# A twice normed input: both norms of the second attention from one set of statistics

## The chip, the cores and the metric

The kernel runs on one core of a Trainium2 chip. Its engines work side by side: TensorE (PE) multiplies, VectorE (DVE), ScalarE (ACT) and GpSimd (POOL) do elementwise work, SyncE (SP) issues the transfers. Each engine takes its instructions in the order of the program, and waits on semaphores that others raise. The time is that of one execution on the device in microseconds; a comparison goes by the median of the runs.

## What is computed

x has 8 batches of 256 rows of 256 numbers. Four blocks follow one another, each adding to x: an attention of x to a context, a block with self attention and a choice among 8 experts, a second attention to the context, and a block of small experts. The change is in the second one:

```python
def _layernorm(x, axis=-1, eps=1e-05):
    m = jnp.mean(x, axis=axis, keepdims=True)
    v = jnp.var(x, axis=axis, keepdims=True)
    return (x - m) / jnp.sqrt(v + eps)
...
    def _L0_ffn_ref(x, ln1_g, ln1_b, ...):
        hn = _layernorm(x, ln1_g, ln1_b)
        q = (hn @ wq + bq)...
        ...
        x = x + (o @ wo + bo)
        ...
        return x + moe.reshape(b, s, h)
    x = x + _L0_ffn_ref(_layernorm(x, axis=-1), ...)
```

So the rows of x are normed (call this y, to which the attention's result is added), and y is normed once more for the projections to queries, keys and values.

## The kernel before

All work stands in one list, `STEPS`, of small steps with a batch number; every engine walks through the list and does its part of each step. Batches 0 to 7 are the first attention, 8 to 15 the self attention, 16 to 23 the second attention to the context. `pipeline` lays out the list: each batch has a few chains of steps with hand written due times (`T_SELF` for the chain that starts a self attention batch), and the attention units of the current batch (`sc` scores, `pv` values) are the clock that the due times refer to. PE's own order is the list's.

The steps that matter here:
- `na` (`norm_stats`, line 1015): on DVE two BN_STATS and two BN_AGGR (one for each tile of 128 rows) and a TENSOR_SCALAR that adds eps to both variances (`ve`); on POOL (line 1312) one TENSOR_TENSOR with the exponent -0.5 in `mhalf`, which makes the two reciprocal roots `rs`. The numbers lie in a ring of three small tiles, `mv`.
- `nb` (`norm_apply`, line 1029): on DVE two TENSOR_SCALAR, (source - mean) * root. `norm_io` gives source and destination. For a self attention batch n, `("nb", n, 0)` writes y from x and `("nb", n, 1)` writes z from y; z is what PE turns (`zt`) and ACT and PE make queries (`qp`), keys (`kp`) and values (`vp`) of.
- `qs` and `ks`: a projection is split into three bf16 parts; POOL subtracts (`rqa`, line 1327), DVE casts (`spa`, line 1050), POOL subtracts again (line 1334), and SP sends the parts to the stacks of queries and keys (line 1473).
- `mx`: PE multiplies queries and keys for the row maxima (line 604), DVE reduces them (`nma`, line 1072). Their results and those of most other steps share a ring of three PSUM banks, so PE's next step often waits for the reduction three back.
- `p0`, `ps`, `p1`, `p2`: reciprocal of the softmax sums (`La`, line 1088), its splitting into bf16 parts (`Lpa`, lines 1094 to 1100), the product that spreads it (line 652), the output projection (line 661) and DVE's addition of it to x or y (line 1113).
- `of`: POOL adds the output bias to x or y (line 1340).

Before, `("nb", n, 0)` and `("na", n, 1)` stand in one segment of the chain, and `("nb", n, 1)` in the next, whose due time is 0.02 of a batch later.

## Time and profile before

| | us |
|---|---|
| median of 3 runs | 949.85 |
| lowest and highest | 948.77, 954.06 |
| the profiled execution | 945.36 |
| its span | 943.6 |

The span by stage, from the busy times by stretch (us; granted clock as a share of 2.4 GHz):

| stretch | what runs | PE busy | DVE busy | POOL busy | clock |
|---|---|---|---|---|---|
| 0 to 126 | first attention, start | 77.5 | 66.6 | 39.4 | 0.84 |
| 126 to 427 | self attention, and the first one's end | 255.4 | 227.9 | 94.3 | 0.94 |
| 427 to 627 | the eight experts | 169.9 | 40.8 | 25.0 | 0.93 |
| 627 to 870 | second attention to the context | 173.3 | 158.8 | 80.5 | 0.75 |
| 870 to 943.6 | small experts, end | 63.7 | 48.2 | 3.6 | 0.96 |

Within the second stage PE is busy for 30.5 of 38 us (126 to 164), 58.6 of 66 (164 to 230) and 77.8 of 87 (230 to 317).

How to read the rows further down: start in us from the span's start, length in us, engine, line of the kernel, operation, destination <- sources, shapes, how many were merged in the row ("x2"), and in brackets how long the engine was idle before it and what ended that. A start can lie a little before the end of the row ahead, since instructions overlap in their pipeline.

### The profile page before, as it was taken

How to read it: one execution, taken by the hardware profiler on the slowest of the kernel's cores; microseconds unless marked ns; L12 is line 12 of the kernel's file. 1: busy time of each engine (PE TensorE's matmuls, PEld its weight loads, DVE VectorE, ACT ScalarE, POOL GpSimd, SP SyncE). 2: the span in 40 equal slices, each digit the busy share in tenths (PEclk: the TensorE clock that was granted, in tenths of full speed). 3: DMA queues.
4: the chain of work that ended last, by engine and by line, in shares of the span. 5: the costliest groups of instructions: out<-in, count | busy, mean ns of one | idle time of the engine just before them, and what ended most of it. 6: DMA issues, size and time to landing. Idle time of an engine off the chain costs nothing.

```text
span 943.6 us, 15777 instructions
## 1 busy us (share of the span) xinstructions
PE 739.9 (78%) x5815; PEld 548.4 (58%) x5815; DVE 542.2 (57%) x1319; ACT 344.2 (36%) x627; POOL 242.7 (26%) x242
## 2 busy tenths in 40 slices
PE   3657878889988999930999999935477768887898
PEld 2434655556555655420999999924354545565775
DVE  3546588987788687442111221125558889465585
ACT  1324454545454455510222222204044444543313
POOL 1513233333333331312111110026233542212000
PEclk9768898999999999965999999978578898665999
DMA  4959364855555484336455566246936442060202
GB/s 149 123 76 199 67 92 71 117 83 82 68 119 63 82 139 155 114 122 145 177 187 198 169 175 181 91 103 75 113 58 90 82 73 42 13 280 13 86 0 91
DMA packets 66191, 102.94 MB, mean 109 GB/s; under 512 B 20078, under 2 KB 56366, under 8 KB 60958
## 3 DMA queue, kind: packets, MB, share of 16 engines
q1 hardware_dynamic: 63699, 96.75, 47.9%
q0 software_dynamic: 2416, 5.19, 3.0%
q8 instruction: 47, 0.77, 0.4%
q14 instruction: 29, 0.24, 0.1%
HBM read 56.29 MB, written 7.28 MB: 67 GB/s over the span
## 4 chain that ended last, share of the span: by engine, by line
PE 53%; DVE 21%; DMA 10%; issue 5%; ACT 5%; POOL 3%; SPq 3%; DVEq 0%; POOLq 0%; ACTq 0%
PE PS L723 9%; PE U L734 8%; PE U L641 6%; PE MB L574 6%; PE MB L661 4%; PE PS L627 4%; PE MB L604 3%; DVE R L1276 3%; DVE nma L1072 3%; DMA La<-Uba 2%; SPq L1473 2%; DMA y<-yb,pos 2%; PE PS L778 2%; DMA QKa<-mTa 2%; PE MB L590 2%
## 5 line engine op out<-in xcount | busy, mean ns | idle before, releaser
L1072 DVE TENSOR_REDUCE nma<-MB 128x2 f32<-128x512 f32 (+1 forms) x192 | 123.9, 671 | 36.9 <-PE MB L604 35.2
L899 ACT ACTIVATE Pa<-PS 128x1024 f32<-128x1024 f32 (+1 forms) x96 | 97.4, 1023 | 65.8 <-PE PS L627 65.2
L604 PE MATMUL MB<-QKa 99*128 99x120 bf16 (+1 forms) x512 | 73.4, 259 | 29.5 <-DVE nma L1072 18.0
L641 PE MATMUL U<-Pa,Vaa 128*32 128x256 f32 (+1 forms) x768 | 91.7, 403 | 0.9 <-ACT Pa L899 0.7
L723 PE MATMUL PS<-mzT,mw 128*128 128x128 f32 x736 | 87.6, 278 | 1.8 <-ACT mzT L921 1.8
L723 PEld LDWEIGHTS PS<-mzT,mw 128*128 128x128 f32 x736 | 85.6, 195 | 2.4 <-issue 2.3
L734 PE MATMUL U<-mw,mdT 128*128 x368 | 83.3, 380 | 2.3 <-DVE mdT L1224 2.3
L1232 DVE TENSOR_TENSOR yt<-U,mb 128x256 f32<-128x256 f32 x23 | 9.8, 424 | 122.7 <-PE U L734 122.7
L1318 POOL TENSOR_TENSOR mv<-mv,vec 128x2 f32<-128x2 f32 x48 | 34.1, 711 | 178.4 <-DVE mv L1027 178.4
L604 PEld LDWEIGHTS MB<-QKa 99*128 99x128 bf16 x512 | 39.3, 103 | 61.9 <-DVE nma L1072 26.8
L734 PEld LDWEIGHTS U<-mw,mdT 128*128 128x128 f32 x368 | 68.2, 190 | 11.0 <-issue 2.7
L627 PE MATMUL PS<-QKa 101*128 101x256 bf16 (+1 forms) x384 | 59.7, 279 | 4.9 <-DMA QKa<-mTa 4.9
L921 ACT ACTIVATE mzT<-MB,vec 128x128 f32<-128x128 f32 x46 | 18.5, 454 | 116.5 <-PE MB L707 116.5
L574 PE MATMUL MB<-zTa,W 128*128 128x256 f32 x192 | 47.9, 393 | 7.5 <-ACT zTa L842 6.1
L1327 POOL TENSOR_TENSOR rqa<-tqa,spa 128x512 f32<-128x512 f32 (+1 forms) x28 | 32.6, 1166 | 81.1 <-ACT tqa L881 38.9
L1365 POOL DMA_INDIRECT zt<-hb,rows_of x23 | 21.7, 945 | 121.8 <-PE MB L707 117.0
L641 PEld LDWEIGHTS U<-Pa,Vaa 128*32 128x32 f32 (+1 forms) x768 | 31.0, 111 | 32.5 <-issue 15.4
L1072 DVE TENSOR_REDUCE nmb<-MB 128x4 f32<-128x480 f32 x64 | 40.7, 651 | 14.4 <-PE MB L604 13.7
L627 PEld LDWEIGHTS PS<-QKa 101*128 101x128 bf16 (+1 forms) x384 | 37.8, 113 | 17.1 <-issue 8.1
L899 ACT ACTIVATE Pb<-PS 120x1024 f32<-120x1024 f32 x32 | 32.7, 1021 | 34.8 <-PE PS L627 34.6
L574 PEld LDWEIGHTS MB<-zTa,W 128*128 128x128 f32 x192 | 35.0, 192 | 16.7 <-ACT zTa L842 7.7
L1334 POOL TENSOR_TENSOR spa<-rqa,spa 128x512 bf16<-128x512 f32 (+1 forms) x28 | 32.5, 1159 | 43.8 <-DVE spa L1050 43.8
(202 smaller groups left out, 1381.1 us busy)
## 6 DMA issues: line engine op xcount, KB each, us to landing
mw<-in_mw SPq DMA_DIRECT2D x31, 1024.0 KB, 5.6
QKa<-spa SPq DMA_DIRECT2D x144, 128.0 KB, 4.7
Qb<-spb SPq DMA_DIRECT2D x48, 128.0 KB, 5.5
Oa<-Uba SPq DMA_DIRECT2D x16, 256.0 KB, 3.8
v<-in_v SPq DMA_DIRECT2D x1, 4096.0 KB, 13.5
v<-in_v SPq DMA_DIRECT2D x4, 1024.0 KB, 11.7
W<-in_W SPq DMA_DIRECT2D x3, 1280.0 KB, 6.6
yb<-yt SPq DMA_DIRECT2D x23, 128.0 KB, 1.7
```

The costliest lines, as they stand in the source:

```text
L574: i = e.matmul(b[:, 256 * half:256 * half + cols], w[:, k, 128 * half:128 * half + 128], rhs[:, k, :], start=k == 0, stop=k == 1)
L604: i = e.matmul(b[:, keys * j:keys * j + keys], Q[0:99, h0 + j, 128 * qt:128 * qt + 128], K[0:99, h0 + j, 0:keys], start=True, stop=True)
L627: i = e.matmul(ps[0:keys, c:c + 256], K[0:101, h, keys * kt:keys * kt + keys], Q[0:101, h, :], start=True, stop=True)
L641: i = e.matmul(U[32 * j:32 * j + 32, 256 * gg:256 * gg + 256], V[0:keys, kt, 8 * half + 4 * gg + j, :], p[0:keys, c:c + 256], start=kt == ...
L661: i = e.matmul(b[:, 256 * tt:256 * tt + 256], o[:, half, 128 * tt:128 * tt + 128], W.o[:, half, :], start=half == 0, stop=half == 1)
L723: i = e.matmul(ps[:, 128 * f:128 * f + 128], w[:, k, 128 * f:128 * f + 128], zz[:, k, :], start=k == 0, stop=k == 1)
L734: i = e.matmul(U[:, 0:256], mdT[j % 2][:, f, :], w2[:, bass.ds(expert[j], 1), f, :], start=f == 0, stop=f == 7)
L899: e.activation(p[0:keys, :], ps[0:keys, :], ACT.Exp, scale=0.25).then_inc(sems["exp"], 1)
L1072: e.tensor_reduce(A.nm[qt][:, h0:h0 + heads], b[:, 0:heads * keys].rearrange("p (h s) -> p h s", h=heads), AX.X, ALU.max, negate=True).the ...
L1318: e.tensor_tensor(rs[r][:, 0:2], ve[r][:, 0:2], mhalf[:, 0:2], ALU.pow).then_inc(sems["rs"], 1)
L1327: e.tensor_tensor(r, f32, hi, ALU.subtract).then_inc(sems["split_r"], 1)
L1334: e.tensor_tensor(low, A.rq[k % 2][:, :, 0:cols], mid_, ALU.subtract).then_inc(sems["split_l"], 1)
```

## The change

With the mean m and the variance v of a row of x, y = (x - m) / sqrt(v + eps) has mean 0 and variance v / (v + eps). Its norm is therefore (x - m) / sqrt(v * (1 + eps) + eps^2). The change takes statistics of x alone for a self attention batch, and makes both y and z from x with them. `("na", n, 1)` is gone; `("na", n, 0)` has one more TENSOR_SCALAR on DVE, which makes the second pair of `ve`, and POOL's power works on four numbers a row instead of two. z (`nb` with 1) now comes first, in the segment where y was made, and y (`nb` with 0) in the next, where z was. `stats_done` and `applied` give the semaphore values that the constant 5 and `k - 2` gave before; `twofold` names the norms that have two users. POOL's bias addition waits for both. All else in the list keeps its place.

```diff
--- before.py
+++ after.py
@@ -83,7 +83,7 @@
             task(at(T_KEYS[L][1:]), [("vp", n)])
             task(at(T_CROSS), [("na", n, 0)], [("nb", n, 0)], [("zt", n)], [("qp", n)], [("qs", n)], [("qd", n), ("of", n)])
         else:
-            task(at(T_SELF), [("na", n, 0)], [("nb", n, 0), ("na", n, 1)], [("nb", n, 1)], [("zt", n)], [("qp", n)],
+            task(at(T_SELF), [("na", n, 0)], [("nb", n, 1)], [("nb", n, 0)], [("zt", n)], [("qp", n)],
                  [("qs", n), ("kp", n)], [("qd", n), ("ks", n)], [("kr", n), ("kd", n), ("vp", n), ("of", n)])
         per = 4 if cross(n) else 8
         segments = []
@@ -246,6 +246,7 @@
 
 PAIRS = Ring(2, score_users())
 NORM = {s[1:]: k for k, s in enumerate(s for s in STEPS if s[0] == "na")}
+NORMS = list(NORM)
 HT = Ring(2, [(s, ("logits", s[1] - 7) if s[0] == "gt" else ("choice", s[1] - 15)) for s in STEPS if s[0] in ("gt", "ft")])
 
 
@@ -296,6 +297,25 @@
 KEY_SENT, KEY_ROWS, KEY_BEFORE = key_uses()
 LOW = {(s[0][0] + "p", s[1]): k for k, s in enumerate(s for s in STEPS if s[0] in ("qs", "ks"))}
 NB_AT = {s[1:]: k + 1 for k, s in enumerate(s for s in STEPS if s[0] == "nb")}
+
+
+def twofold(n, i):
+
+
+    return i == 0 and not cross(n)
+
+
+def stats_done(k):
+
+    return sum(6 if twofold(*s) else 5 for s in NORMS[:k])
+
+
+def applied(k):
+
+    n, i = NORMS[k]
+    return max(NB_AT[n, i], NB_AT[n, 1] if twofold(n, i) else 0)
+
+
 Z_STEPS = [s[1] for s in STEPS if s[0] == "zt"]
 
 
@@ -347,11 +367,11 @@
     vec = g0.new("vec", [128, 160])
     cst = g0.new("cst", [128, 176])
     lo = g0.new("lo", [128, 2, 128], BF)
-    mhalf = vec[:, 136:138]
+    mhalf = vec[:, 136:140]
     st = g0.ring("st", 3, [128, 2, 6])
-    mvs = g0.ring("mv", 3, [128, 8])
+    mvs = g0.ring("mv", 3, [128, 12])
     mv = [t[:, 0:4].rearrange("p (n m) -> p n m", n=2) for t in mvs]
-    ve, rs = [t[:, 4:6] for t in mvs], [t[:, 6:8] for t in mvs]
+    ve, rs = [t[:, 4:8] for t in mvs], [t[:, 8:12] for t in mvs]
     oh = g0.new("oh", [128, NT, 8])
     gw = g0.new("gw", [128, 2, 8])
     hT = g0.ring("ghT", 2, [128, 2, 256])
@@ -532,7 +552,7 @@
         if i == 0:
             ready = ((f"d_x{b}", 16), ("resid", NO["p2"].get((n - 8,), 0)), ("back", b + 1))[layer(n)]
         else:
-            ready = (None, ("nb", NORM[n, 0] + 1), ("resid", NO["p2"].get((n,), 0)), ("resid", NO["p2"].get((n,), 0)))[i]
+            ready = ("resid", NO["p2"].get((n,), 0))
         if (i == 0 and cross(n)) or i == 1:
             z = att(n).z[z_of(n) % 2]
             dst = [z[:, k, :] for k in range(2)]
@@ -540,7 +560,7 @@
             dst = [Yz[b % 2][:, k, :] for k in range(2)]
         else:
             dst = ys
-        return (xs if i in (0, 3) else ys), dst, ready
+        return (ys if i == 2 else xs), dst, ready
 
     def normed(n):
         return "nb", NB_AT[n, 0 if cross(n) else 1]
@@ -1016,18 +1036,23 @@
             k = NORM[n, i]
             r = k % 3
             src, _, ready = norm_io(n, i)
+            done = stats_done(k)
             g.wait_ge(*ready)
-            g.wait_ge("nb", k - 2)
+            if k >= 3:
+                g.wait_ge("nb", applied(k - 3))
             for t in range(2):
                 e.bn_stats(st[r][:, t, :], src[t]).then_inc(sems["na"], 1)
             for t in range(2):
-                g.wait_ge("na", 5 * k + 1 + t)
+                g.wait_ge("na", done + 1 + t)
                 e.bn_aggr(mv[r][:, t, :], st[r][:, t, :]).then_inc(sems["na"], 1)
-            g.wait_ge("na", 5 * k + 4)
+            g.wait_ge("na", done + 4)
             e.tensor_scalar(ve[r][:, 0:2], mv[r][:, 0:2, 1], EPS, None, ALU.add).then_inc(sems["na"], 1)
+            if twofold(n, i):
+                e.tensor_scalar(ve[r][:, 2:4], mv[r][:, 0:2, 1], 1.0 + EPS, EPS * EPS, ALU.mult, ALU.add
+                                ).then_inc(sems["na"], 1)
 
         def norm_apply(n, i):
-            k = NORM[n, i]
+            k = NORM[n, 0 if i == 1 else i]
             r = k % 3
             src, dst, _ = norm_io(n, i)
             if (i == 0 and cross(n)) or i == 1:
@@ -1040,7 +1065,8 @@
                 g.wait_ge("fl", n - 17)
             g.wait_ge("rs", k + 1)
             for t in range(2):
-                o = e.tensor_scalar(dst[t], src[t], mv[r][:, t, 0:1], rs[r][:, t:t + 1], ALU.subtract, ALU.mult)
+                w = 2 + t if i == 1 else t
+                o = e.tensor_scalar(dst[t], src[t], mv[r][:, t, 0:1], rs[r][:, w:w + 1], ALU.subtract, ALU.mult)
             o.then_inc(sems["nb"], 1)
 
         def split_mid(what, n):
@@ -1313,9 +1339,11 @@
             k = NORM[n, i]
             r = k % 3
             g.wait_ge("mhalf", 1)
-            g.wait_ge("nb", k - 2)
-            g.wait_ge("na", 5 * k + 5)
-            e.tensor_tensor(rs[r][:, 0:2], ve[r][:, 0:2], mhalf[:, 0:2], ALU.pow).then_inc(sems["rs"], 1)
+            if k >= 3:
+                g.wait_ge("nb", applied(k - 3))
+            g.wait_ge("na", stats_done(k + 1))
+            w = 4 if twofold(n, i) else 2
+            e.tensor_tensor(rs[r][:, 0:w], ve[r][:, 0:w], mhalf[:, 0:w], ALU.pow).then_inc(sems["rs"], 1)
 
         def split_rest(what, n):
             A, k = att(n), SPLIT[what, n]
@@ -1336,7 +1364,7 @@
         def offset(n):
             res = (x if cross(n) else y)[:, two(n % NB), :]
             g.wait_ge(f"d_W{layer(n)}", 16)
-            g.wait_ge(*normed(n))
+            g.wait_ge("nb", max(NB_AT[n, 0], normed(n)[1]))
             e.tensor_tensor(res, res, over(LW[layer(n)].bo, 2, 1), ALU.add).then_inc(sems["offset"], 1)
 
         def add_y(n):
```

DVE at the start of batch 8, before (`x` and `y` are the residual tiles, `za` is z, `st` the statistics, `mv` the ring of means, variances and roots):

```order
L1072 TENSOR_REDUCE nma_85<-MB 128x4
L1081 CAST Mha_90<-nma_86 128x16
L1083 TENSOR_TENSOR Mha_90<-nma_86,Mha_90 128x16
L1043 TENSOR_SCALAR y<-x,mv_61 128x256 x2
L1022 BN_STATS st_56<-y 128x6 x2
L1025 BN_AGGR mv_59<-st_56 128x2 x2
L1027 TENSOR_SCALAR mv_59<-mv_59 128x2
L1050 CAST spa_107<-rqa_103 128x512
L1043 TENSOR_SCALAR za_96<-y,mv_59 128x256 x2
L1072 TENSOR_REDUCE nma_85<-MB 128x4
```

and in the changed kernel:

```order
L1098 TENSOR_REDUCE nma_85<-MB 128x4
L1107 CAST Mha_90<-nma_86 128x16
L1109 TENSOR_TENSOR Mha_90<-nma_86,Mha_90 128x16
L1069 TENSOR_SCALAR za_96<-x,mv_61 128x256 x2
L1076 CAST spa_107<-rqa_103 128x512
L1069 TENSOR_SCALAR y<-x,mv_61 128x256 x2
L1098 TENSOR_REDUCE nma_85<-MB 128x4
```

The pair that writes za has moved up to the first pair's place and reads x; the statistics of y are gone, and the pair that writes y stands behind the cast.

POOL there, before (`mv` is the power, `rqa` and `spa` the two subtractions of a split):

```order
L1318 TENSOR_TENSOR mv_61<-mv_61,vec 128x2
L1327 TENSOR_TENSOR rqa_103<-tqa_101,spa_107 128x512
L1318 TENSOR_TENSOR mv_59<-mv_59,vec 128x2
L1334 TENSOR_TENSOR spa_107<-rqa_103,spa_107 128x512
L1340 TENSOR_TENSOR x<-x,W_74 128x512
```

and in the changed kernel:

```order
L1346 TENSOR_TENSOR mv_61<-mv_61,vec 128x4
L1355 TENSOR_TENSOR rqa_103<-tqa_101,spa_107 128x512
L1362 TENSOR_TENSOR spa_107<-rqa_103,spa_107 128x512
L1368 TENSOR_TENSOR x<-x,W_74 128x512
```

The second power, between the two subtractions, is gone, and the first has four columns.

DVE at batch 13, where the splitting of the softmax sums (`La`, `Lpa`) stands between the two pairs, before:

```order
L1088 RECIPROCAL La_82<-La_82 32x128
L1043 TENSOR_SCALAR y<-x,mv_59 128x256 x2
L1022 BN_STATS st_57<-y 128x6 x2
L1025 BN_AGGR mv_60<-st_57 128x2 x2
L1027 TENSOR_SCALAR mv_60<-mv_60 128x2
L1094 CAST Lpa_94<-La_82 32x128
L1096 TENSOR_TENSOR La_82<-La_82,Lpa_94 32x128
L1098 CAST Lpa_94<-La_82 32x128
L1100 TENSOR_TENSOR Lpa_94<-La_82,Lpa_94 32x128
L1050 CAST spa_104<-rqa_102 128x512
L1043 TENSOR_SCALAR za_97<-y,mv_60 128x256 x2
L1072 TENSOR_REDUCE nma_85<-MB 128x2
```

and in the changed kernel:

```order
L1114 RECIPROCAL La_82<-La_82 32x128
L1069 TENSOR_SCALAR za_97<-x,mv_60 128x256 x2
L1120 CAST Lpa_94<-La_82 32x128
L1122 TENSOR_TENSOR La_82<-La_82,Lpa_94 32x128
L1124 CAST Lpa_94<-La_82 32x128
L1126 TENSOR_TENSOR Lpa_94<-La_82,Lpa_94 32x128
L1076 CAST spa_104<-rqa_102 128x512
L1069 TENSOR_SCALAR y<-x,mv_60 128x256 x2
L1098 TENSOR_REDUCE nma_85<-MB 128x2
```

Here the four instructions of the sums come right behind the pair that writes za. PE's, ACT's and SP's orders are the same in both kernels.

## Rows read from the trace of the kernel before

**Rows 1.** Timeline of DVE at batch 8 (start us, us, operation, idle before).

```profile
132.86 1.65 DVE L1043 TENSOR_SCALAR y<-x,mv 128x256 f32<-128x256 f32 x2
134.55 0.75 DVE L1022 BATCH_NORM_STATS2 st<-y 128x6 f32<-128x256 f32 x2
...
135.55 0.17 DVE L1027 TENSOR_SCALAR mv<-mv 128x2 f32<-128x2 f32 x1
135.63 0.42 DVE L1050 CAST spa<-rqa 128x512 bf16<-128x512 f32 x1
136.70 2.42 DVE L1043 TENSOR_SCALAR za<-y,mv 128x256 f32<-128x256 f32 x2 [0.65 <-POOL mv L1318]
139.05 0.64 DVE L1072 TENSOR_REDUCE nma<-MB 128x4 f32<-128x480 f32 x1
```

**Rows 2.** The same of POOL at batch 8, and its first bias addition to y.

```profile
135.80 0.80 POOL L1318 TENSOR_TENSOR mv<-mv,vec 128x2 f32<-128x2 f32 x1 [1.43 <-DVE mv L1027]
136.56 1.15 POOL L1334 TENSOR_TENSOR spa<-rqa,spa 128x512 bf16<-128x512 f32 x1
137.67 1.30 POOL L1340 TENSOR_TENSOR x<-x,W 128x512 f32<-128x512 f32 x1
...
162.77 1.27 POOL L1340 TENSOR_TENSOR y<-y,W 128x512 f32<-128x512 f32 x1
```

**Rows 3.** Timeline at batch 13: DVE, last row POOL.

```profile
238.98 0.75 DVE L1022 BATCH_NORM_STATS2 st<-y 128x6 f32<-128x256 f32 x2
...
240.06 0.21 DVE L1094 CAST Lpa<-La 32x128 bf16<-32x128 f32 x1
...
241.22 0.43 DVE L1050 CAST spa<-rqa 128x512 bf16<-128x512 f32 x1
241.57 1.57 DVE L1043 TENSOR_SCALAR za<-y,mv 128x256 f32<-128x256 f32 x2
243.05 0.68 DVE L1072 TENSOR_REDUCE nma<-MB 128x2 f32<-128x512 f32 x1
...
241.73 1.25 POOL L1334 TENSOR_TENSOR spa<-rqa,spa 128x512 bf16<-128x512 f32 x1 [0.75 <-DVE spa L1050]
```

**Rows 4.** Timeline at batch 10: DVE, then POOL.

```profile
168.61 0.73 DVE L1043 TENSOR_SCALAR y<-x,mv 128x256 f32<-128x256 f32 x2
...
170.45 0.42 DVE L1050 CAST spa<-rqa 128x512 bf16<-128x512 f32 x1
...
173.77 1.27 DVE L1072 TENSOR_REDUCE nma<-MB 128x2 f32<-128x512 f32 x2
...
167.53 0.70 POOL L1318 TENSOR_TENSOR mv<-mv,vec 128x2 f32<-128x2 f32 x1 [3.48 <-DVE mv L1027]
169.17 1.18 POOL L1327 TENSOR_TENSOR rqa<-tqa,spa 128x512 f32<-128x512 f32 x1 [0.95 <-ACT tqa L884]
```

**Rows 5.** Timeline of PE: rows that carry a wait, batches 8, 9, 10, 13.

```profile
139.75 0.38 PE L604 MATMUL MB<-QKa 99*128 99x120 bf16 x4 [3.20 <-DVE nma L1072]
...
159.60 1.99 PE L590 MATMUL MB<-W,zTa 128*128 128x256 f32 x8 [0.57 <-DVE x L1113]
...
172.11 0.60 PE L604 MATMUL MB<-QKa 99*128 99x256 bf16 x4 [1.39 <-issue]
...
243.78 3.50 PE L661 MATMUL MB<-W,Oa 128*128 128x256 f32 x8 [1.48 <-DVE nma L1072]
```

**Rows 6.** Timeline at batches 11 and 12: DVE, DVE, PE.

```profile
196.82 0.69 DVE L1113 TENSOR_TENSOR x<-x,MB 128x512 f32<-128x512 f32 x1 [0.17 <-PE MB L661]
...
216.09 1.27 DVE L1072 TENSOR_REDUCE nma<-MB 128x2 f32<-128x512 f32 x2
...
216.27 1.90 PE L661 MATMUL MB<-W,Oa 128*128 128x256 f32 x8
```

**Rows 7.** Second attention to the context: busy times by stretch (engines, clock, DMA); one product, ns min/median/max.

```profile
627.00:850.00 223.00, 157.84 (x1204) 110.92 (x1206) 147.62 (x329) 88.64 (x149) 77.45 (x75) 0.77 0.50 94
...
L574 PE MATMUL MB<-zTb,W x40: 378/379/748, 642.7 to 707.5; 128*128 128x256 f32 x40
```

## Prediction

> **What bounds the kernel now.** I read the busy time by stretch first, then TensorE's (PE's) rows that carry a wait, then the rows of VectorE (DVE) and GpSimd (POOL) at each place the diff touches. The change is confined to the second stretch of the table above, the self attention of batches 8 to 15, whose eight double norms start between 132.9 and 299.4 us. The other stretches stand before or behind it and are not touched; in its three parts named under the table, PE is busy for 80 to 89%. So the question is how much of the work taken from DVE lies on the way to PE's next product.
>
> Batch 8 is the clearest place [rows 1]. DVE makes y from x with the first norm (132.86), takes statistics of y (from 134.55), adds eps (135.55), does an unrelated cast (135.63), and makes za, the second norm of y, from 136.70 on: between the cast and za it stands 0.65 us, until POOL's power (135.80 plus 0.80) is there [rows 2]. Only then can it do the maximum at 139.05. PE has no other work: its row at 139.75 shows 3.20 us of waiting for that maximum [rows 5]. The pair za takes 2.42 us, where an undisturbed pair of this shape takes 0.73 (168.61) [rows 4]: it runs while POOL has two subtractions or additions back to back, 136.56 and 137.67 [rows 2].
>
> Batch 13 shows the other pattern [rows 3]. There the four splitting steps of the softmax sums stand between, so the power is ready in time, and the pair za meets one POOL operation (241.73) before it gets through: from the cast's start (241.22) to the next maximum (243.05) 1.83 us pass. PE waits 1.48 us for that maximum in its row at 243.78 [rows 5]; the rows at 275.88 and 304.95, for batches 14 and 15, carry the same 1.48.
>
> **What is removed.** Per batch two BN_STATS, two BN_AGGR and one TENSOR_SCALAR go. They occupy DVE from 134.55 to 135.63, that is 1.08 us [rows 1]; in batch 13 from 238.98 to 240.06, again 1.08 [rows 3]. The stop for the second power goes as well: the two reciprocal roots come out of one POOL operation, issued over 3 us earlier in batch 8. Eight POOL operations of 0.70 to 0.80 us go, which nobody but DVE waited for.
>
> **What moves.** za takes the place of the first pair, and y that of the second, behind the cast. The first pair keeps its price. The second now starts right behind the cast, with no power in POOL's queue, which is how batches 13 to 15 already run, so I price it by their 1.83 us from cast to maximum. In batch 8 the same distance is 135.63 to 139.05, 3.42 us [rows 1]: 1.59 are saved. In batch 10 it is 170.45 to 173.77, 3.32 us [rows 4], and the rows of batch 9 have the same 3.32: 1.49 are saved in each.
>
> **Batch by batch**, what DVE gains and what PE can take of it:
> - Batch 8: 1.08 + 1.59 = 2.67 us. PE stood 3.20 us for it, so all of it counts: **2.67**.
> - Batch 9: DVE gains 1.08 + 1.49 = 2.57, but PE's own product keeps it busy, and behind it the row at 159.60 waits only 0.57 for DVE's residual addition [rows 5], and one before it 0.18 for a maximum. I take both, **0.75**; the bounds are 0.57 and 2.57.
> - Batch 10: the cast needs POOL's subtraction, 169.17 plus 1.18 = 170.35 [rows 4], so it can only move from 170.45 to about 170.40; 0.05 + 1.49 = 1.54. DVE runs from there almost without a stop, and PE's row at 172.11 has 1.39 us of waiting that no engine is named for. I read it as the landing of batch 8's keys, sent after a cast that DVE now reaches sooner. **1.5**.
> - Batches 11 and 12: the next thing that DVE must do is an addition for which PE's product is late: at 196.82 it waits 0.17 for PE in spite of everything; in batch 12 the product runs from 216.27 to 218.17, while DVE comes to the same addition over maxima that start at 216.09 and take 1.27 and a reciprocal of about 0.9 [rows 6], so just in time. What DVE gains (1.73 and 0.7 by the same working) ends in a wait for PE. **0**.
> - Batches 13, 14, 15: no stop for the power, the cast-to-maximum distance is unchanged, so 1.08 each, and PE stands 1.48 for each: **3.24**.
>
> Sum 2.67 + 0.75 + 1.5 + 3.24 = 8.16 us.
>
> **What is added.** One TENSOR_SCALAR on 128x2 beside the one that adds eps. The existing one is 0.17 us long and the next instruction starts 0.08 behind it when it does not depend on it (135.55, 135.63) [rows 1]. Eight such are 0.6 us of DVE at most 1.4; about half of them lie where DVE is what PE waits for: 0.3. The power works on four numbers a row, not two. No row has that shape: its bounds are 0.70, if its time is all fixed cost, and 1.40, if it is all work. The tightest place is batch 10, power at 167.53, pair at 168.61 [rows 4]: 0.70 hides, 1.40 would hold the pair 0.3 us. I take nothing, since 0.70 for two numbers against 1.15 for the 512 of 136.56 says fixed cost. The addition of the output bias to y (POOL) now waits for y behind za; the first comes at 162.77, 24 us after both pairs [rows 2], so this costs nothing. Rings with fewer users and earlier frees cost nothing.
>
> So **8.16 - 0.3 = 7.9 us**. The profiled execution took 945.36 us, so it would take 937.5. The median of the runs is 949.85; the profiled one is 4.5 below it, and the same saving in each gives **941.9**.
>
> **Where the pair y could come out dearer.** In rows 3 the pair starts 0.16 us ahead of POOL's subtraction and meets one POOL operation; in batch 8 POOL was first and both halves of the pair waited, one operation each. If POOL came first in batches 8 to 10, only the stop of 0.65 would be saved behind the cast, not 1.59 and 1.49: 0.94 + 0.84 + 0.84 = 2.6 less, a gain of 5.3. The Trainium skill (SBUF — State Buffer, Who interferes with whom) says that a VectorE instruction in a two-port mode and a GpSimd one share a port pair that the first to start holds for its whole length; with the pair at the front in all three batches that gives the sum above, with POOL at the front the smaller gain. The trace agrees with it on both patterns, 2.42 and 1.57 us for the pair. I keep 1.83 because both POOL's operation and the pair are released by the same cast, and POOL needs a signal for it while DVE only goes on.
>
> **The rivals.**
> - *The saving is taken back by others* (0 to 4.5 us gained, 945.4 to 949.9). PE is busy for most of this stage; wherever it comes early, it may find the next keys not landed, as in the row at 172.11, or ScalarE not done. If batches 9 and 10 give nothing and 13 to 15 give half, 2.67 + 1.6 = 4.3 us, 945.6. For it: two of eight batches give nothing already in my own reckoning. Against: the 1.48 and 3.20 us are waits for DVE alone.
> - *More comes through* (12.1 us, 937.8). Batch 9 gives its full 2.57 and batches 11 and 12 their 1.73 and 0.7: 7.9 + 1.8 + 2.4 = 12.1. It needs PE's waits on ScalarE to fall too. Against: DVE's own rows wait for PE there.
> - *Slower by the clock of the second attention to the context.* That stretch runs at a mean granted clock of 0.77 [rows 7], switching between the levels 1.2 and 2.4 GHz, and the same product takes 0.379 us at one and up to 0.748 at the other [rows 7]. The change moves this stage by some 8 us against whatever sets the switching. It decides once about 8 us of PE work more fall to the lower level, some 16 us of its 223, a mean clock near 0.70; at 0.65 the result is 5 to 6 us slower, 955. For it: a clock that goes up and down here many times. Against: fewer waits ahead of it, and no work changed in it.
> - That the change does not do what it says can be left out: the order of DVE shows the five instructions gone and PE's order is the same.
>
> **Chances.** Forecast, 5 to 9.5 us gained: 0.48. Taken back: 0.27. More: 0.16. Slower: 0.09. A measurement can tell about 0.5%, 4.7 us, from no change. Faster by more than that: the forecast, more, and a sliver of the second case, 0.66. Same: 0.27. Slower, at a little under the last case: 0.07. The range reaches from the large gain to a gain of 1.4: 937.5 to 948.5; below it and above it I leave about 0.2.
>
> **What will show it.** In the profile after: no statistics of y in front of za, and no wait of DVE for POOL's power in batches 8 to 12; PE's wait of 3.20 in batch 8 down to about 0.5; the three waits of 1.48 down to 0.4; cast to maximum 1.8 us in batches 8 to 10, and the power of 128x4 near 0.7 us. The end of the stage (the last product of the router, near 423 us) should be 8 us earlier, and the stretch behind it as long as before. The forecast is wrong if those waits turn up under ScalarE or a transfer, if the pair y takes 2.4 us, or if the second half is longer at a lower clock.

## The result and the profile after

The changed kernel took 939.14 us (median of 4 runs, 933.67 to 941.93) against 949.31 before (4 runs, 947.75 to 954.06); the ratio is 0.9889, with a 95% interval of 0.9854 to 0.9923. A second set of runs of the same kernel gave 0.993 (0.9895 to 0.9966; 12 runs against 35). Both intervals lie below 1; the medians are 10.2 and 6.3 us apart, and the forecast was 7.9. The two profiled executions of the changed kernel, though, have spans of 931.9 and 944.8 us, so a single profile's total says little here. What can be compared is how long a piece of the program takes in each profile.

DVE at batch 8 in the profile after, the columns as ahead of the prediction; it answers [rows 1]:

```profile
132.85 0.73 DVE L1069 TENSOR_SCALAR za<-x,mv 128x256 f32<-128x256 f32 x2
134.62 0.43 DVE L1076 CAST spa<-rqa 128x512 bf16<-128x512 f32 x1 [1.05 <-POOL rqa L1355]
134.97 1.57 DVE L1069 TENSOR_SCALAR y<-x,mv 128x256 f32<-128x256 f32 x2
136.46 0.65 DVE L1098 TENSOR_REDUCE nma<-MB 128x4 f32<-128x480 f32 x1
```

The pair that writes za stands first and is undisturbed, 0.73 us. The cast now waits 1.05 us for POOL's first subtraction, which nothing hides any more; the pair y takes 1.57 us, and the maximum follows 1.8 us behind the cast instead of 3.42. The power with four columns, and the first row of PE behind all this, which was [rows 5]'s 139.75 with its 3.20 us:

```profile
129.65 1.02 POOL L1346 TENSOR_TENSOR mv<-mv,vec 128x4 f32<-128x4 f32 x1 [6.25 <-DVE mv L1051]
...
137.16 0.38 PE L624 MATMUL MB<-QKa 99*128 99x120 bf16 x4 [0.63 <-DVE nma L1098]
```

The power takes 1.02 us, between the bounds of 0.70 and 1.40, and delays nobody here. At batch 10, where it is tightest, it ends at 164.34 and the pair starts at 164.45, after 0.11 us of idle time. PE's wait is 0.63. At batch 13 (DVE, POOL, PE; [rows 3] and the last of [rows 5] answer to it):

```profile
235.27 1.36 DVE L1069 TENSOR_SCALAR za<-x,mv 128x256 f32<-128x256 f32 x2
236.56 0.21 DVE L1120 CAST Lpa<-La 32x128 bf16<-32x128 f32 x1
...
237.68 0.43 DVE L1076 CAST spa<-rqa 128x512 bf16<-128x512 f32 x1
238.02 1.57 DVE L1069 TENSOR_SCALAR y<-x,mv 128x256 f32<-128x256 f32 x2
239.51 0.68 DVE L1098 TENSOR_REDUCE nma<-MB 128x2 f32<-128x512 f32 x1
...
238.18 1.26 POOL L1362 TENSOR_TENSOR spa<-rqa,spa 128x512 bf16<-128x512 f32 x1 [2.02 <-DVE spa L1076]
...
240.25 1.99 PE L681 MATMUL MB<-W,Oa 128*128 128x256 f32 x8 [0.59 <-DVE nma L1098]
```

The splitting of the sums starts right behind the pair za. PE's wait for the maximum fell from 1.48 to 0.59 us, and its projection in the same row from 3.50 to 1.99. That second fall was in no term of the sum. The waits for the maximum in batches 14 and 15 fell less, from 1.48 to 1.04 and 0.98 (269.67 and 297.54); 0.4 was forecast for all three.

At batch 10, on PE, where [rows 5] has 1.39 us at 172.11:

```profile
168.97 1.01 PE L624 MATMUL MB<-QKa 99*128 99x256 bf16 x4 [2.59 <-issue]
```

This wait has grown to 2.59 us. It was to shrink.

**One table for all kernels.** Each kernel's first product of the softmax sums with `Lpa` (line 652 before; it belongs to batch 4, and stands at 125 to 130 us) is taken as zero, since the start alone differs by 5 us between executions. Times in us. "To batch 13" ends at the same product of batch 10's sums, six products further; in the profile of before it stands at 241.25 us, 2.5 ahead of the wait of 1.48 in batch 13, so it holds what batches 8 to 12 gave. "13 to 15" is from there to the product three further, past the third such wait; "experts" is the first product of the experts' stage; "rest" is what follows the last expert product to the end of the span.

| kernel | first maxima product of batch 8 | to batch 13 | "13 to 15" | experts | rest | ratio to before (95%) |
|---|---|---|---|---|---|---|
| before | 47.09 | 116.2 | 90.0 | 323.5 | 323.3 | |
| changed, first profile | 43.89 | 113.2 | 84.2 | 315.9 | 318.7 | 0.9889 (0.9854, 0.9923) |
| changed, `again` | 45.34 | 115.9 | 84.3 | 318.1 | 323.6 | 0.993 (0.9895, 0.9966) |
| `y_first` | 45.41 | 113.2 | 84.2 | 315.0 | 322.6 | 0.9914 (0.9878, 0.995) |
| `dummy_stats` | 46.17 | 116.2 | 89.9 | 324.6 | 323.0 | 0.9998 (0.9965, 1.0031) |
| `second_power` | 46.12 | 115.5 | 84.2 | 318.5 | 322.9 | 0.9976 (0.9946, 1.0005) |
| `only_13_15` | 46.75 | 115.3 | 84.2 | 317.3 | 323.2 | 0.9956 (0.9926, 0.9986) |
| `only_8_10` | 45.22 | 113.6 | 89.7 | 320.5 | 317.3 | 0.9956 (0.9917, 0.9995) |
| `only_11_12` | 46.62 | 115.8 | 90.2 | 323.5 | 323.4 | 1.0013 (0.9978, 1.0048) |
| `keys_sooner` | 45.53 | 113.3 | 84.2 | 314.7 | 317.9 | one run, 937.75 us |
| `y_later` | 43.96 | 113.5 | 84.9 | 318.3 | 323.2 | 0.993 (0.9891, 0.997) |
| `eight_sooner` | 44.10 | 114.9 | 87.8 | 320.8 | 324.0 | 0.9928 (0.9887, 0.9968) |
| `both_moves` | 42.88 | 112.1 | 84.4 | 314.2 | 324.2 | 0.9925 (0.9891, 0.9959) |

The column "rest" has two values, 317 to 319 and 322.6 to 324.2, in kernels whose work there is the same, and the changed kernel shows both. The 5 us lie in the last two batches of the second attention to the context: between the products of the last three batches' softmax sums pass 11.5 and 16.9 us in the first profile after and 13.2 and 20.5 in `before` and in `again`, and the clock differs there. So the difference between the two executions of the changed kernel is not the change's. The experts' stage itself, from its first product to its last, is in no column and has two values too: 171.7 to 172.3 us in `before`, the first profile after and the three kernels with the new way in some batches only, and 174.1 to 174.8 in the eight others, the second execution of the changed kernel among them. Whether the change makes the longer value more frequent, no run here shows; `before` was profiled once.

Up to the experts, the two executions of the changed kernel are 7.6 and 5.4 us ahead of before. They differ by 2.7 us ahead of batch 13. There the granted clock is at 1.2 GHz for 13.7 us in `again`, counted from the product at zero (two of the stretches begin at 175.5 and 192.5 us), and for 6.8 us in the first profile (one begins at 168.6). In `before`, `y_first`, `y_later`, `keys_sooner`, `eight_sooner` and the three kernels with the new way in some batches only it is 6.8 us as well, in `dummy_stats` and `second_power` 10.2, in `both_moves` 3.4. So of single profiles a difference under some 3 us in that column says little unless these times are the same; the column "13 to 15" repeats within 0.1.

### The profile page after: what moved, and what is told of

Read it like the earlier page. It is cut to its first block, busy times and chain, and to the rows that moved or that the text cites. A ratio compares the mean times of both kernels' runs of the same rounds, so it can differ in the third digit from the quotient of the medians.

```text
span 931.9 us, 15736 instructions
## 1 busy us (share of the span) xinstructions
PE 731.7 (79%) x5815; PEld 543.8 (58%) x5815; DVE 532.9 (57%) x1287; ACT 344.3 (37%) x627; POOL 240.7 (26%) x234
## 4 chain that ended last, share of the span: by engine, by line
PE 54%; DVE 20%; DMA 8%; issue 5%; ACT 5%; SPq 3%; POOL 3%; DVEq 0%; POOLq 0%; ACTq 0%
PE PS L743 9%; PE U L754 9%; PE U L661 7%; PE MB L594 6%; PE MB L681 4%; PE PS L647 4%; PE MB L624 3%; DVE R L1302 3%; DVE nma L1098 2%; SPq L1501 2%; DMA y<-yb,pos 2%; DMA QKa<-mTa 2%; PE MB L610 2%; PE MB L833 2%; PE PS L798 2%
## 5 line engine op out<-in xcount | busy, mean ns | idle before, releaser
L1346 POOL TENSOR_TENSOR mv<-mv,vec 128x2 f32<-128x2 f32 (+1 forms) x40 | 31.1, 777 | 156.3 <-DVE mv L1049 105.4
L661 PEld LDWEIGHTS U<-Pa,Vaa 128*32 128x32 f32 (+1 forms) x768 | 30.7, 110 | 31.7 <-issue 14.2
```

Source lines behind the costliest of these rows:

```text
L661: i = e.matmul(U[32 * j:32 * j + 32, 256 * gg:256 * gg + 256], V[0:keys, kt, 8 * half + 4 * gg + j, :], p[0:keys, c:c + 256], start=kt == ...
L1346: e.tensor_tensor(rs[r][:, 0:w], ve[r][:, 0:w], mhalf[:, 0:w], ALU.pow).then_inc(sems["rs"], 1)
```

## The experiments

### Which part of the removal counts

`again` is the changed kernel.

> The changed kernel once more, unaltered. In its first profile the stretch up to the experts' start was 7.1 to 8.3 us shorter than before (PE's last router transposition at 409.09 instead of 417.39), and the rest of the span 3.4 to 4.6 us shorter as well, although no work there is changed. Theory A (the change is worth what its stage shows, about 8 us, and the rest is how the clock of the second context attention fell in that one execution): the stage ends again near 409 to 410, the total lands 7 to 11 us under the kernel before, and the rest of the span differs from 522 us by a few us. Theory B (the later stages gain too): the rest is again near 522 us and the total 10 to 12 us under.

It took 942.37 us against 948.7. Its stage ended 5.8 us earlier than the kernel before, counted from the product at zero (277.4 instead of 283.2), or 5.4 at the experts, and its rest was 323.6: theory A, though the gain in the total, 6.3 us, lies below its 7 to 11. The expected absolute times were of no use, since the start shifts.

`dummy_stats` puts the five DVE instructions back, with unused results:

```diff
-            task(at(T_SELF), [("na", n, 0)], [("nb", n, 1)], [("nb", n, 0)], [("zt", n)], [("qp", n)],
+            task(at(T_SELF), [("na", n, 0)], [("nb", n, 1), ("dm", n)], [("nb", n, 0)], [("zt", n)], [("qp", n)],
...
+        def dummy(n):
...
+                e.bn_stats(s[t], x[:, 2 * (n % NB) + t, :]).then_inc(sems["dummy"], 1)
...
+                e.bn_aggr(m[:, t, :], s[t]).then_inc(sems["dummy"], 1)
...
+            e.tensor_scalar(vec[:, 156:158], m[:, 0:2, 1], EPS, None, ALU.add).then_inc(sems["dummy"], 1)
```

> The changed kernel with five VectorE instructions put back behind each pair that writes z: two BN_STATS and two BN_AGGR and a TENSOR_SCALAR into unused columns, read by nobody. No second power on GpSimd. It prices the removed instructions apart from the removed stop. My theory: they cost 1.08 us per batch, in full in batches 8, 10, 13, 14 and 15 and not in 11 and 12, so the stage ends 5 us later than in the changed kernel (near 414), total about 944. The rival (the stop for the power was what mattered, the five instructions run in the shadow of PE): the stage ends within 1.5 us of 409. In batch 8 PE's first maxima product stands at 138.2 by my theory, at 137.2 by the rival.

With the five back, nothing measurable is left: 948.29 us against 948.7, where about 944 was expected, and the experts start 1.1 us later than before, although the stop for the second power is gone and the second pair is cheaper. Part of that can be the clock: ahead of batch 13 this profile has 3.4 us more at 1.2 GHz than before, which at half the speed is at most 1.7 us. DVE at batch 8:

```profile
134.29 1.69 DVE L1069 TENSOR_SCALAR za<-x,mv 128x256 f32<-128x256 f32 x2
135.91 0.74 DVE L1077 BATCH_NORM_STATS2 vec<-x 128x6 f32<-128x256 f32 x2
136.57 0.29 DVE L1080 BATCH_NORM_AGGREGATE vec<-vec 128x2 f32<-128x6 f32 x2
136.89 0.17 DVE L1082 TENSOR_SCALAR vec<-vec 128x2 f32<-128x2 f32 x1
136.97 0.42 DVE L1088 CAST spa<-rqa 128x512 bf16<-128x512 f32 x1
137.31 1.57 DVE L1069 TENSOR_SCALAR y<-x,mv 128x256 f32<-128x256 f32 x2
138.80 0.64 DVE L1110 TENSOR_REDUCE nma<-MB 128x4 f32<-128x480 f32 x1
```

The instructions cost 1.06 us, from 135.91 to 136.97, as priced, and from the cast on the batch is as cheap as in the changed kernel (1.83 us to the maximum, 3.42 before). PE's first maxima product behind it stands 0.94 us later than in the changed kernel, counted from the zero, as expected, but by the rows the reason is the first pair, which took 1.69 us beside POOL's subtraction: after a pair of 0.73 the five would have been done at about 136.0, and the cast needs that subtraction, which ends at 135.84. So the price of 1.59 us for stop and contention was right in its place, and worth nothing measurable at the end. That contradicts the share of it in my sum: of 7 to 8 us I expected 5 to go, and all went.

`second_power` is the other half: statistics once, but y first, one TENSOR_SCALAR where the five stood, and the second power on POOL ahead of z.

```diff
+            task(at(T_SELF), [("na", n, 0)], [("nb", n, 0), ("pw", n)], [("nb", n, 1)], [("zt", n)], [("qp", n)],
...
+        def second_variance(n):
...
+            e.tensor_scalar(ve[r][:, 2:4], mv[r][:, 0:2, 1], 1.0 + EPS, EPS * EPS, ALU.mult, ALU.add
...
+        def second_power(n):
...
+            e.tensor_tensor(rs[r][:, 2:4], ve[r][:, 2:4], mhalf[:, 2:4], ALU.pow).then_inc(sems["pw_a"], 1)
```

> Statistics of x alone, as in the changed kernel, but order and power as before: y first, then one TENSOR_SCALAR for the second variance where the five instructions stood, then the second power on GpSimd, then z behind the cast. It takes away four instructions (about 1.0 us per batch) and keeps the stop. My theory: batches 8 and 10 gain only about 1 us each, 13 to 15 about 1.0 each, so the stage ends near 412.5 (4 to 5 us before the kernel before, 3 to 4 behind the changed one). The rival (the stop is worth nothing because it hides under PE): it ends near 409, like the changed kernel. In batch 8 the maximum starts 3.4 us after the cast, not 1.8.

Of DVE at batch 8:

```profile
135.38 0.43 DVE L1080 CAST spa<-rqa 128x512 bf16<-128x512 f32 x1 [1.23 <-POOL rqa L1364]
136.10 2.43 DVE L1068 TENSOR_SCALAR za<-x,mv 128x256 f32<-128x256 f32 x2 [0.30 <-POOL mv L1355]
138.45 0.65 DVE L1102 TENSOR_REDUCE nma<-MB 128x4 f32<-128x480 f32 x1
```

The stop is 0.30 us here and the pair takes 2.43, with POOL busy throughout; cast to maximum is 3.07 us, where 3.4 was expected. It comes to batch 13 at 115.5, about where `again` does, so nothing can be read from that; and its stage ends at 276.5, between the two executions of the changed kernel (274.8 and 277.4), which decides for neither theory. But batches 13 to 15 take 84.2 us, as in the changed kernel. At the experts it is 5.0 us ahead; its total is 2.3 us ahead with an interval that reaches from 5.1 ahead to 0.5 behind, so the total alone settles nothing. The four removed instructions are all that counts in batches 13 to 15.

`y_first` swaps the two pairs back.

> The changed kernel with only the order of the two pairs swapped back: y in the first place, z in the second, behind the cast. Nobody takes z before PE's transposition, whose place in PE's order is some 5 us later. My theory: the order is worth nothing, the stage ends within 0.5 us of the changed kernel's 409.1. The rival (z's being ready earlier is part of the gain): it ends 1 us or more later.

It comes to batch 13 at 113.2 and takes 84.2 us from there, like the first profile of the changed kernel; the ratio is 0.9914. The order of the two is worth nothing, as expected: both pairs read x, so neither needs the other.

### Batch by batch

The changed kernel with the new way for some batches only (`ONCE` holds them; the others are as before):

```diff
+ONCE = (13, 14, 15)
...
+            first_, second_ = ([("nb", n, 1)], [("nb", n, 0)]) if n in ONCE else ([("nb", n, 0), ("na", n, 1)], [("nb", n, 1)])
...
-    return i == 0 and not cross(n)
+    return i == 0 and n in ONCE
```

> Only batches 13, 14 and 15 take both norms from x; batches 8 to 12 are as before. Times are counted from PE's first product of softmax sums with Lpa (batch 4, near 125 us), since the start varies by some us. Theory A (the granted clock doubles the gain here: the waits of 1.5 us that go had each been followed by a half-clock stretch): up to the product of batch 10 it is like before, 116.2 us, and the last one is at 277.4 instead of 283.2, 5.8 us earlier, against the 3.24 of the prediction; the half-clock stretches that the profile of before records at 254.9 and 316.3 are gone. Theory B (the gain there is only the instructions): 280.0, and the two half-clock stretches stay.

> Only batches 8, 9 and 10 take both norms from x. Counted from the same product. The prediction's sum would be 4.9 us. Theory A (in batches 8 to 10 the transfers of the first self attention queries and keys take it back: 15.7 us from the first send of the queries of batch 8 to the first maxima product of batch 8, whatever the engines do): 0.4 to 3.1 us at the product of batch 10 (116.2 before), and the half-clock stretches near 255 and 316 stay, so the total is 0 to 3 us under before. Theory B: 4 us or more.

> Only batches 11 and 12 take both norms from x. My theory: nothing, since VectorE waits for PE's projection there anyway: the product of batch 10 at 116.2 us and the last at 283.2 from the first, each within 0.5, total within 1 us of before. The rival (the slack of the two is smaller than it looks): 1 us or more at the product of batch 10.

Batches 13 to 15 alone take "13 to 15" from 90.0 to 84.2 us, 5.8, against the 3.24 of the sum. Batches 11 and 12 alone give 0.0 at the experts. Batches 8 to 10 alone come to batch 13 at 113.6, against 116.2, 115.3 and 115.8 in the three profiles with the old way in these batches and the same 6.8 us at 1.2 GHz: 1.7 to 2.7 us, against the 4.9 of the sum. Five of the six profiles with the whole change in batch 8 and its old place lie between 113.2 and 113.6, only `again`, with its 13.7 us at the lower clock, at 115.9. In all three runs the first of the two theories holds for the gain. The places that the expectations give for the stretches at 1.2 GHz were read wrongly: counted from the start of the span, as all rows here are, they begin at 243.4 and 304.9 us in the profile of before, not at 254.9 and 316.3, so at the ends of the waits at 243.78 and 304.95. The wait at 275.88 has none.

**Why 5.8.** PE at batch 13 in `dummy_stats`, where the wait is as before, and in `only_13_15`:

```profile
245.21 3.56 PE L681 MATMUL MB<-W,Oa 128*128 128x256 f32 x8 [1.48 <-DVE nma L1110]
```

```profile
245.37 1.99 PE L683 MATMUL MB<-W,Oa 128*128 128x256 f32 x8 [0.59 <-DVE nma L1100]
```

The same eight products take 3.56 us behind the wait of 1.48, and 1.99 behind one of 0.59. Around batch 15, a product with the values behind the last of the three waits (PE, `dummy_stats`, then `only_13_15`):

```profile
306.60 1.93 PE L661 MATMUL U<-Pa,Vaa 128*32 128x256 f32 x8
```

```profile
306.77 1.06 PE L663 MATMUL U<-Pa,Vaa 128*32 128x256 f32 x8
```

1.93 us against 1.06. It is the clock. The granted clock by stretch (columns: stretch, its length, busy time and count of PE, PE's weight loads, DVE, ACT and POOL, granted clock, DMA share, GB/s), in `dummy_stats`, first of the two stretches behind the waits, then of wider ones:

```profile
245.00:248.40 3.40, 3.19 (x8) 2.56 (x9) 1.35 (x3) 0.00 (x0) 0.57 (x1) 0.50 0.76 131
306.40:309.80 3.40, 3.40 (x20) 1.60 (x18) 2.55 (x9) 0.60 (x1) 0.18 (x1) 0.50 0.89 143
...
229.00:263.00 34.00, 31.71 (x215) 20.20 (x213) 25.26 (x60) 15.77 (x25) 9.03 (x8) 0.95 0.47 67
290.00:325.00 35.00, 31.77 (x222) 20.30 (x217) 26.68 (x72) 16.73 (x26) 11.01 (x10) 0.95 0.56 81
```

The wider ones in `second_power`:

```profile
229.00:263.00 34.00, 32.60 (x227) 20.73 (x224) 26.38 (x61) 16.36 (x25) 10.09 (x10) 1.00 0.47 79
290.00:325.00 35.00, 32.70 (x238) 21.96 (x238) 26.75 (x72) 19.25 (x33) 11.81 (x11) 1.00 0.49 75
```

A share of 0.50 is 1.2 GHz, one of 0.95 over 34 or 35 us a stretch of 3.4 us at 1.2 GHz, the rest at 2.4. Before, in `dummy_stats` and in `only_11_12` there is one in each of these windows; in `second_power`, `only_13_15`, `y_first`, `keys_sooner`, `y_later`, `both_moves` and both executions of the changed kernel there is none. `only_8_10`, with the waits still 1.48, has one in the middle instead, of double length:

```profile
276.10:282.90 6.80, 6.28 (x25) 3.76 (x26) 3.91 (x11) 1.72 (x3) 2.50 (x3) 0.50 0.87 116
```

Of the twelve waits of 1.48 or 1.49 us in these four profiles seven have such a stretch behind them and five have none. Of the kernels without these waits only `eight_sooner` has one (294.8 us, 6.8 long), behind a wait of 1.59 us for ACT.

Since `only_8_10` has the stretch elsewhere, the work and the clock can be priced apart. The time between the four products that bound "13 to 15", in us:

| kernel | first | second | third |
|---|---|---|---|
| before | 32.1, with a stretch of 3.4 us | 29.1 | 28.8, with a stretch of 3.4 us |
| `only_8_10` | 30.6 | 31.7, with a stretch of 6.8 us | 27.4 |
| changed | 29.0 | 27.9 | 27.3 |

Without a low stretch on either side the removed work is worth 1.6, 1.1 and 0.2 us, 2.9 together; the two stretches of before are worth 1.5 and 1.4, again 2.9. Together that is the 5.8. It rests on one profile of `only_8_10`. I did not take the waits away while keeping the five instructions, so waits and the instructions that make them were never parted.

### What takes the gain of batches 8 to 10

PE's wait ahead of the first maxima product of batch 8 grew from 1.39 to 2.59 us. I held that DVE's cast of the keys decided it. `keys_sooner` does this cast for batch 8 three instructions and more sooner:

```diff
+            soon = n == 8
+            task(at(T_SELF[:6] + ((-2.49,) if soon else ()) + T_SELF[6:]), [("na", n, 0)], [("nb", n, 1)], [("nb", n, 0)],
+                 [("zt", n)], [("qp", n)], [("qs", n), ("kp", n)], *([[("ks", n)], [("qd", n)]] if soon else [[("qd", n), ("ks", n)]]),
```

> The changed kernel, but for batch 8 VectorE's cast of the keys comes 3 us sooner, ahead of its addition for batch 3. PE stands 2.6 us for these keys before its first maxima product of batch 8. Theory A (the 16 DMA engines are full from the first send of the queries on, and 12 transfers of 128 KB take 15.7 us): the keys' sends start 0.7 us sooner and PE's wait stays at 2.6, the product 15.7 us behind the first send of the queries. Theory B (the landing follows the last send): the wait falls by 0.7 us or more.

SP's sends of queries and keys, and PE's product that needs them, in `after`:

```profile
153.27 3.82 SPq L1501 DMA_DIRECT2D QKa<-spa  x6
...
158.36 3.81 SPq L1501 DMA_DIRECT2D QKa<-spa  x6
...
168.97 1.01 PE L624 MATMUL MB<-QKa 99*128 99x256 bf16 x4 [2.59 <-issue]
```

and in `keys_sooner`:

```profile
158.48 3.81 SPq L1503 DMA_DIRECT2D QKa<-spa  x6
...
162.87 3.81 SPq L1503 DMA_DIRECT2D QKa<-spa  x6
...
174.25 0.60 PE L626 MATMUL MB<-QKa 99*128 99x256 bf16 x4 [2.36 <-issue]
```

From the first send to the product pass 15.70 us in the one and 15.77 in the other, though the keys' sends follow after 5.1 and 4.4 us. PE's wait is 2.36 us, where theory A had 2.6 and theory B 1.9 or less. In the nine other profiles with this order on SP (before, `again`, and all but the two that move batch 8) it is 15.64 to 15.80. In between the DMA engines are full, here in `after`:

```profile
156.00:159.00 3.00, 2.64 (x24) 2.16 (x26) 2.90 (x8) 1.85 (x3) 1.83 (x2) 1.00 1.16 124
159.00:162.00 3.00, 3.00 (x33) 1.95 (x28) 2.97 (x6) 1.58 (x3) 0.56 (x1) 1.00 1.16 125
162.00:165.00 3.00, 3.00 (x25) 2.14 (x24) 2.77 (x12) 1.91 (x6) 1.20 (x2) 1.00 1.16 126
```

The transfers land one by one, about 1.1 us apart, the twelfth at 168.88 in `after` and at 174.16 in `keys_sooner`, and PE's product starts 0.09 us behind it in both; SP also sends 256 KB for `Oa` in between (162.92 in `after`). So the twelve transfers decide, from the first one on, and how soon DVE casts the keys does not. What the change gave here is what it moved the first send: 31.3 us behind the zero before (30.8 and 31.0 in `only_11_12` and `only_13_15`), 28.2 to 29.8 in the six profiles with the whole change in batch 8, 30.4 in `dummy_stats` and in `second_power`. Of the six, the two at 28.2 (`after`, `y_later`) have 3.4 us at 1.2 GHz between the zero and this send, the four at 29.6 to 29.8 have 6.8, as before and the others have; so at the same clock the change moved it by 1.1 to 1.8 us. That also fits the cheaper pair of `dummy_stats`, which ended at nothing: its first send is only 0.4 to 0.9 us sooner.

### Two tries at more

`y_later` moves y one maximum later (`T_SELF` with -3.5 in place of -3.61). `eight_sooner` moves all of batch 8's chain up:

```diff
-        e = EARLY[m] if m < 3 else m
+        e = m - 0.4 if n == 8 else EARLY[m] if m < 3 else m
```

> The changed kernel with y, which nobody needs soon, made one maximum later in batches 11 and 13 to 15: PE stood 0.6, 1.0 and 1.0 us there for the maximum that follows the pair. My theory: the maximum comes 1.5 us sooner and these waits vanish, but VectorE is late by the same 1.5 us after it, so PE takes 0.3 to 1.0 us per batch: 1 to 3 us between the products of batches 10 and 13 (84.2 us in the changed kernel). The rival: PE waits for the next reduction instead, 84.2 within 0.3.

> The changed kernel with the whole chain of batch 8, from its norm to the sending of keys, 0.4 of a batch sooner in the list. PE stood 2.6 us for the landing of these keys, 15.7 us behind the first send of the queries with all DMA engines full. My theory: the sends start some 7 us sooner, the 15.7 us overlap other work, the wait of 2.6 us vanishes, and with it the half-clock stretch behind it: 2.5 to 4 us at the product of batch 10 (113.2 in the changed kernel, from the first one), so 109 to 110.7. The rival: another wait (the ring of projections, keys of batch 7, or a transfer that is now in the way) takes its place, less than 1 us.

> Both moves at once, against the kernel before. If they are independent, the last product with Lpa comes at 274.8 less their sum, 269 to 272 us from the first one, and the total 1.2 to 1.6% under before. If the earlier work of batch 8 fills VectorE, less than the larger of the two.

`y_later` needs 84.9 us for "13 to 15", 0.7 more than the changed kernel, where 1 to 3 less were expected: PE then stands for the step behind the pair. At batch 14:

```profile
271.94 0.17 PE L711 MATMUL MB<-ohb,lo 128*128 128x24 bf16 x1 [0.98 <-DVE Oa L1132]
...
272.45 0.39 PE L624 MATMUL MB<-QKa 99*128 99x256 bf16 x2 [0.30 <-DVE nma L1098]
```

My theory fell there. In `eight_sooner` the wait of 2.59 is gone, and others have come (PE):

```profile
143.26 0.39 PE L624 MATMUL MB<-QKa 99*128 99x120 bf16 x4 [0.71 <-ACT tqa L904]
...
148.33 0.37 PE L624 MATMUL MB<-QKa 99*128 99x120 bf16 x4 [1.39 <-ACT tqa L904]
...
154.68 3.68 PE L681 MATMUL MB<-W,Oa 128*128 128x256 f32 x8 [1.29 <-DVE Vaa L1086]
```

0.71 and 1.39 us for ACT's splitting, then 1.29 for DVE, with a projection of 3.68 us behind it. It comes to batch 13 at 114.9, no better than the changed kernel, where 109 to 110.7 was expected. `both_moves` came there at 112.1 and to the experts at 314.2, the least of all, but its stage ended at 273.4 and not at 269 to 272, and its ratio of 0.9925 (0.9891 to 0.9959) is that of the changed kernel. No version is measurably better than the change itself.

## Why the prediction was right

The total was right: 7.9 us forecast, 10.2 and 6.3 measured, and 7.6 and 5.4 up to the experts in the two profiles. The sum behind it holds two errors that nearly cancel, one term too large by 2.2 to 3.2 us and one too small by 2.6. That the total fits as well as it does is in part luck.

- **The removed instructions, 1.08 us per batch: right.** 1.06 in `dummy_stats`, where they can be seen put back. That is their length; what it is worth differs by place.
- **The second pair at 1.83 us from cast to maximum, with DVE ahead of POOL: right** in batch 8 (134.62 to 136.46) as in batch 13 (237.68 to 239.51). The case in which POOL comes first shows in `second_power`, 3.07 us with a stop of 0.30. The Trainium skill (SBUF — State Buffer, Who interferes with whom) has a DVE instruction in a two-port mode and a POOL one exclude each other at a shared pair of ports; the rows agree, 0.73 us for a pair alone, 1.57 beside one POOL operation, 2.43 beside two.
- **Batch 8, 2.67 us: too large.** From the table's zero to the same product of batch 5, which lies behind batch 8's norm, it is 15.7 to 15.8 us in the kernels with the change there (but 16.4 in `eight_sooner`, 16.8 and 16.9 in `dummy_stats` and `second_power`), 18.5 in the profile of before and 17.4 in the two others with the old batch 8 (`only_11_12`, `only_13_15`). PE's wait was 3.20 in the one and 2.17 in `only_11_12`. So 1.6 us is nearer the mark than 2.67. The rows say why: the profile of before had a dear first pair, 1.65 us [rows 1], and in `only_11_12` and `only_13_15` the same pair took 0.73. And the five instructions were almost free here: counted from the start of the first pair, the cast starts after 1.84 us in `only_11_12` and after 1.77 in the changed kernel, where it waits 1.05 us for POOL's first subtraction. The prediction saw this limit for batch 10 and not for batch 8. What batch 8 gained is the 1.6 us between cast and maximum.
- **Batches 9 and 10, 0.75 and 1.5: the step that failed.** "I read it as the landing of batch 8's keys, sent after a cast that DVE now reaches sooner": the landing it was, but not the cast. The twelve transfers, with the DMA engines full, take 15.7 us from the first on, and PE, now early, stands 1.2 us longer for them. Batches 8 to 10 together gave 1.7 to 2.7 us in `only_8_10`, not 4.9. It is what the rival of the saving taken back describes, for this part.
- **Batches 11 and 12, nothing: right** (`only_11_12`, 1.0013 and 0.0 us at the experts).
- **Batches 13 to 15, 3.24 us: mis-sized, 5.8.** The mechanism was right, PE stood for DVE alone, and the work was worth 2.9 us; the term left out that behind two of the three waits PE ran at 1.2 GHz for 3.4 us each, which cost another 2.9 together. [Rows 5] had the sign of it: the projection behind the wait took 3.50 us, and the same one takes 1.9 to 2.0 elsewhere, as at 216.27 in [rows 6].
- **The added TENSOR_SCALAR, 0.3 us, and the power of four columns:** the power takes 1.02 us instead of 0.70, hidden but for 0.11 us at batch 10. The extra instruction takes 0.16 us and the next one starts 0.07 behind it (129.41 and 129.48); what it is worth was not measured by itself.
- **The clock of the second attention to the context:** both kinds of "rest" occur in the same kernel, so a single profile shows nothing of the change there, and whether the change alters how often each occurs was not measured. The 5 us between them are at least half the effect, and the interval of the runs has to carry them. The mean clock in that rival was also summed wrongly: 16 us of 223 moved from 2.4 to 1.2 GHz lower it from 0.77 to 0.73, not to 0.70, and 0.65 would be 54 us moved, more than the 5 to 6 us slower that it was given.

The slower rival did not come. The range of 937.5 to 948.5 held both measured medians, 939.14 and 942.37.

## What to carry to other kernels

When DVE is what PE waits for, look at the PE row behind the wait as well as at the wait: if it is twice as long as its like, the wait costs more than it shows, and so does the work that makes it; here that held for seven waits of twelve. When a transfer is what PE waits for, count from the first issue of its group, not the last, and check whether the DMA engines are full in between; if they are, an earlier last issue alone buys nothing. Statistics of an already normed row never need a second pass, and if the first pass's place has slack, the second one's removal is worth what stood behind it.

## What was not expected of the hardware

- The granted clock falls behind some waits of 1.5 us and not behind others, in the same place of nearly the same kernel. Of the twelve waits of 1.48 or 1.49 us seven had a stretch at 1.2 GHz behind them, which began within 0.6 us of the wait's end (in `dummy_stats` the wait ends at 245.21 us and the stretch begins at 245.0). Of the eight waits of 2.36 to 2.66 us ahead of batch 8's first maxima product, five had one (`after`, `again`, `dummy_stats`, `second_power`, `y_later`). What decides it is open.
- POOL's power takes 0.70 us for two columns and 1.02 for four: 0.16 a column, so nearly half the price of two columns is work.
- Twelve transfers of 128 KB between tiles took 15.6 to 15.8 us from the first issue to the product that needs them in eleven profiles, with the second half of the issues starting 4.4 to 6.5 us behind the first.
